# Attention scores of a cycle split three and one around P.V, in place of two and two

## Chip, cores and metric

One NeuronCore of a Trainium2 chip runs the whole program. The metric is the device time of one execution in microseconds (us). Engines are named PE (TensorE matmuls), PEld (its weight loads), ACT (ScalarE), DVE (VectorE), POOL (GpSimd) and SP (SyncE, which here only issues DMAs).

## What is computed

The reference takes x of 8 x 2048 tokens with 256 features and applies three residual blocks: half a routed feed-forward block on 128 picked tokens, an attention over all tokens, and the routed block again. The change touches the attention alone:

```
xh = x.reshape(b, s, 8, 32)                       # after a layer norm
q, k, v = lowrank(xh, Uq, Vq, bq), lowrank(...k), lowrank(...v)
scores = einsum('bqhd,bkhd->bhqk', q, k) / 32 ** 0.5
attn = softmax(scores, axis=-1)
out = einsum('bhqk,bkhd->bqhd', attn, v)
```

Everything is float32.

## The kernel before, in words

The function `attend` (line 1293) works in 64 units, 8 for each of 8 batches. A unit is 4 heads and 512 query tokens, against all 2048 keys. The keys come in 16 chunks of 128. A unit therefore has 64 score tiles, numbered j = 0 to 63, each a matmul of 128 keys by 512 queries for one head (function `score`, matmul on line 1792). Four tiles, the four heads of one chunk, make a **cycle**, and 16 cycles make a unit.

For each tile:

- PE writes the score to one of three PSUM banks (`ps_s`, `RINGS = 3`, line 1261 ff.). The function `score_banks` (line 1264) deals the banks out in turn when the program is written, and remembers for each user who had the bank before (`AFTER`). `after_last` (line 1719) makes PE wait for that user: for an ordinary tile j this is the exponential of tile j - 3.
- ACT takes the exponential of the tile into SBUF (`probs`, line 1682).
- When all four heads of chunk i - 1 are there, PE multiplies them with the values and adds into `ps_acc` (function `pv`, line 1761, eight matmul instructions). It waits for the exponential of tile 4i - 1, the last tile of the cycle before.
- POOL adds the exponentials of the chunks up (`pool_sum`, line 1541), partly after DMAs that add one chunk onto another (line 1520).

Beside this, in each cycle, PE makes four scores of a later unit only for their maximum (`max_four`, line 1795, matmuls on line 1715, four at once in four row groups). DVE reduces three of them (line 1571), ACT copies the fourth out of PSUM (`copy_max`, line 1634) and DVE reduces the copy (line 1573).

The order on PE is written out by hand. In cycle i it is: score(j), score(j + 1), then P.V of chunk i - 1, then score(j + 2), score(j + 3), then the four max scores, with j = 4i. Engines take their instructions in this order, so a waiting instruction holds all behind it. Some cycles carry more:

- Cycle 0: P.V is that of the last chunk of the previous unit. ACT then copies the finished `ps_acc` (`copy_acc`, line 1669), which it does behind the exponential of tile 1. P.V of cycle 1 waits for this copy.
- Cycle 6 (`CLOSE_IN`): behind P.V, PE sums the previous unit's `pool_sum` over the partitions into a bank of `ps_s` (`close_z`, line 1771), for which it waits for POOL's last addition. ACT copies the sums (`copy_z`, line 1675), behind the exponential of tile 25, and PE transposes that copy behind its last score of the cycle (`turn_z`, line 1778). DVE inverts them (line 1586).
- Cycle 7 (`NORM_IN`): behind P.V, PE transposes the copied accumulator (`turn_o`, line 1785), and DVE scales it (line 1602). The bank is held from cycle 6 until tile 34, so that scores turn over in two banks for a while.
- Cycle 13 (`TURN_MAX_IN`): behind the first two scores PE transposes the next unit's maxima (`turn_max`, line 1733) into a bank, and ACT copies them (line 1641).

In the last unit no max scores are left to make, since they run ahead by four cycles and a unit.

Of the kernel before, what the change touches and what calls it, by code (L numbers as in the profile page):

```python
# [1253 lines left out]
NCYC = 16  # L1254
# [3 lines left out]
CLOSE_IN = 6  # L1258
NORM_IN = 7
TURN_MAX_IN = 13  # L1260
RINGS = 3


def score_banks(units, tiles, per_cyc):

    order, last, bank, after = list(range(RINGS)), {}, {}, {}

    def use(user, k):
        bank[user], after[user], last[k] = k, last.get(k), user

    def take(user):
        k = order.pop(0)
        order.append(k)
        use(user, k)

    take((-1, "m"))
    for unit in range(units):  # L1280
        for j in range(tiles):
            if unit > 0 and j == CLOSE_IN * per_cyc + 2:
                use((unit, "z"), order.pop(0))
            if unit > 0 and j == (NORM_IN + 1) * per_cyc + 2:
                order.insert(0, bank[unit, "z"])
            take((unit, j))
            if unit + 1 < units and j == TURN_MAX_IN * per_cyc + 1:
                take((unit, "m"))
    use((units, "z"), order[0])
    return bank, after  # L1290


def attend(nc, tag, qk, v_dram, out):
# [18 lines left out]
    PER_CYC = TILES // NCYC  # L1312
# [5 lines left out]
    ADDS = len(pool_chunks) - 1  # L1318
    ND = len(DMA_PAIRS)
    BANK, AFTER = score_banks(B * BU, TILES, PER_CYC)  # L1320

    def slot(unit, c):

        return (unit * NC + c) % RING

    def adds_through(c):

        return max(pool_chunks.index(c), 1)

    with ExitStack() as ctx:  # L1330
# [5 lines left out]
        def psum(name, shape):  # L1336
            return ctx.enter_context(nc.psum_tensor(f"{tag}_{name}", shape, F32))
# [21 lines left out]
        ps_max = psum("ps_max", [P, HG, 512])  # L1359
        ps_s = psum("ps_s", [P, RINGS, UQ])  # L1360
        ps_acc = psum("ps_acc", [P, UQ])


        def ps_close(unit):

            return ps_s[:, BANK[unit + 1, "z"]]
# [260 lines left out]
        @block.scalar  # L1627
        def _(act):
            def copy_max(unit, n, first_unit=False):

                act.wait_ge(max_scores, unit * FOURS + n + 1)
                if n >= 2 or not first_unit:
                    act.wait_ge(part_max_done, unit * FOURS + n - 1)
                nc.scalar.copy(max_copy[:, n % 2], ps_max[:, HG - 1]).then_inc(max_copied, 1)  # L1634

            def row_of_max(unit, first_unit=False):
                act.wait_ge(max_turned, unit + 1)
                if not first_unit:

                    act.wait_ge(max_in, unit * 32)  # L1640
                nc.scalar.copy(max_row[:], ps_s[0:HG * QT, BANK[unit - 1, "m"], 0:P]).then_inc(max_row_done, 1)

            for n in range(FOURS):
                copy_max(0, n, first_unit=True)
            row_of_max(0, first_unit=True)
            for n in range(MAX_LEAD):
                copy_max(1, n)

            def batch(b, first_batch=False, last=False):
                for un in range(BU):  # L1650
                    unit = b * BU + un
                    carry = un > 0 or not first_batch

                    def free(c):

                        before, k = divmod(unit * NC + c - RING, NC)
                        act.wait_ge(pv_done, before * NC + k + 1)
                        if k in pool_chunks:
                            act.wait_ge(pool_added, before * ADDS + adds_through(k))
                        if k in dma_sources:  # L1660
                            d = before * ND + dma_sources.index(k)
                            act.wait_ge(dma_added[d % MERGES_OUT], (d // MERGES_OUT + 1) * 16)

                    def copy_acc(n):
                        act.wait_ge(pv_done, n * NC)
                        if un > 1 or not first_batch:

                            act.wait_ge(o_turned, n - 1)
                        nc.scalar.copy(oT[:], ps_acc[:]).then_inc(oT_done, 1)

                    def copy_z(n):
                        act.wait_ge(z_done, n)
                        if un > 1 or not first_batch:
                            act.wait_ge(z_turned, n - 1)
                        nc.scalar.copy(zT[:], ps_close(n - 1)).then_inc(zT_done, 1)

                    for j in range(TILES):
                        c, h = divmod(j, HG)
                        if h == 0 and (carry or c >= RING):
                            free(c)  # L1680
                        act.wait_ge(scores, unit * TILES + j + 1)
                        nc.scalar.activation(probs[:, slot(unit, c), h], ps_s[:, BANK[unit, j]], ACT.Exp, scale=SCALE  # L1682
                                             ).then_inc(exp_done, 1)
                        if carry and j == 1:
                            copy_acc(unit)
                        if carry and j == CLOSE_IN * PER_CYC + 1:
                            copy_z(unit)
                        if j == TURN_MAX_IN * PER_CYC + 1 and (un + 1 < BU or not last):
                            row_of_max(unit + 1)
                        if h == HG - 1:  # L1690
                            ahead = un + 1 + (c + MAX_LEAD) // FOURS
                            if ahead < BU or not last:
                                copy_max(unit + ahead - un, (c + MAX_LEAD) % FOURS)
                if last:
                    copy_acc(b * BU + BU)
                    copy_z(b * BU + BU)

            batch(0, first_batch=True)
            for b in range(1, B - 1):
                batch(b)  # L1700
            batch(B - 1, last=True)


        @block.tensor
        def _(pe):
# [13 lines left out]
            def after_last(unit, w):  # L1719

                if AFTER[unit, w] is None:
                    return
                before, x = AFTER[unit, w]
                if x == "z":
                    pe.wait_ge(o_done, before)
                elif x == "m":
                    pe.wait_ge(max_row_done, before + 2)
                else:
                    pe.wait_ge(exp_done, before * TILES + x + 1)

            def turn_max(unit):
                pe.wait_ge(neg_max_done, unit + 1)
                nc.tensor.transpose(ps_s[0:HG * QT, BANK[unit - 1, "m"], 0:P], neg_max[:], ident[:]).then_inc(max_turned, 1)
# [14 lines left out]
            def batch(b, first_batch=False, last=False):  # L1748
                for un in range(BU):
                    unit = b * BU + un  # L1750
                    carry = un > 0 or not first_batch
# [36 lines left out]
                    def score(j):  # L1788
                        c, h = divmod(j, HG)
                        rows = slice(0, LAST_ROW[h])  # L1790
                        after_last(unit, j)
                        nc.tensor.matmul(ps_s[:, BANK[unit, j]], ks[rows, g, h, c * P:(c + 1) * P], qs[rows, unit % NQB, h, :],  # L1792
                                         start=True, stop=True).then_inc(scores, 1)
# [15 lines left out]
                    pe.wait_ge(max_in, unit * 32 + 32)  # L1809
                    for i in range(NCYC):  # L1810
                        j = i * PER_CYC
                        score(j)
                        score(j + 1)
                        if i == TURN_MAX_IN and turns:
                            after_last(unit, "m")
                            turn_max(unit + 1)
                        if i > 0:
                            pe.wait_ge(exp_done, unit * TILES + j)
                            pv(unit, un, i - 1)
                        elif carry:  # L1820
                            pe.wait_ge(exp_done, unit * TILES)
                            pv(unit - 1, (un - 1) % BU, NC - 1)
                        if carry and i == CLOSE_IN:
                            close_z(unit - 1, (un - 1) % BU)
                        if carry and i == NORM_IN:
                            turn_o(unit)
                        score(j + 2)
                        score(j + 3)
                        if carry and i == CLOSE_IN:
                            turn_z(unit)  # L1830
                        max_four(i)
# [8 lines left out]
            for b in range(1, B - 1):  # L1840
                batch(b)
# [60 lines left out]
```

## Time and profile before

| | |
|---|---|
| median of 3 runs | 4373.87 us (4372.24 to 4378.55) |
| the profiled execution | 4375.15 us |
| its span, first to last instruction | 4373.6 us |
| mean granted clock of TensorE | 0.935 |
| busy over the span: PE, DVE, ACT, POOL | 3589.1, 3267.7, 3208.9, 2938.5 us |
| scores, line 1792: PE busy | 1523.4 us in 4096 matmuls |
| P.V, line 1761: PE busy | 1091.8 us in 8192 matmuls |
| exponentials, line 1682: ACT busy | 2262.1 us in 4096 |

The attention's units run from about 830 to 3820 us of the span. Busy time is the union of the recorded instructions of an engine; ends of matmuls are modelled, so a busy PE may still have room. "Idle before" is the time an engine stood still ahead of an instruction, with what ended it. That attribution is inferred: an instruction that waited for a semaphore is put down to whoever raised it, even where it had been raised long before. A row of the time-ordered view begins with the start and the length in us; equal instructions that follow each other are merged into one row with their count.

### The profile page before, as it was taken

What the parts mean: (1) busy time and instruction counts of PE and PEld (TensorE: products, weight loads), DVE (VectorE), ACT (ScalarE), POOL (GpSimd) and SP (SyncE); (2) the same over time, 40 slices, a digit from 0 to 9 for tenths busy, and PEclk for the clock granted to TensorE, in tenths of its full rate; (3) what the DMA queues carried; (4) which work ended last, traced back from release to release, by engine and by line L of the source; (5) the groups of instructions that cost most, each with busy time, mean ns of one, the idle gap of its engine ahead of it and who ended that gap; (6) DMA issues with size and microseconds to landing.
All of it is one profiled execution on the core that took longest, in us unless ns stands there. A gap on an engine that the chain in (4) does not pass through costs nothing. (4 is left out here: it accounts for less than half of the span.)

```text
span 4373.6 us, 59760 instructions
## 1 busy us (share of the span) xinstructions
PE 3589.1 (82%) x20178; PEld 1423.8 (33%) x20178; DVE 3267.7 (75%) x4504; ACT 3208.9 (73%) x6587; POOL 2938.5 (67%) x1094
## 2 busy tenths in 40 slices
PE   0167685599999999999999999999999999900376
PEld 0133463233333333333333333333333333300243
DVE  9644575788888888888888888888888888368544
ACT  5044474498898998998998898998988988723143
POOL 0011000399999999999999999999999999952211
PEclk9998898699999999999999999999999999955588
DMA  8200699689999999999999999999999998877100
GB/s 280 89 3 5 212 395 341 130 180 192 208 199 205 206 199 205 198 209 203 200 208 195 207 198 205 206 199 207 197 208 204 201 205 186 169 249 249 39 5 5
DMA packets 335171, 809.45 MB, mean 185 GB/s; under 512 B 27084, under 2 KB 210912, under 8 KB 271136
## 3 DMA queue, kind: packets, MB, share of 16 engines
q0 software_dynamic: 66432, 475.04, 53.9%
q1 hardware_dynamic: 222496, 284.46, 22.2%
q10 hardware_dynamic: 45952, 46.27, 3.0%
q8 instruction: 159, 2.61, 0.2%
q14 instruction: 132, 1.08, 0.1%
HBM read 198.90 MB, written 136.48 MB: 77 GB/s over the span
## 5 line engine op out<-in xcount | busy, mean ns | idle before, releaser
L1682 ACT ACTIVATE at_probs<-at_ps_s 128x512 f32<-128x512 f32 x4096 | 2262.1, 615 | 254.7 <-PE at_ps_s L1792 247.3
L1541 POOL TENSOR_TENSOR at_pool_sum<-at_pool_sum,at_probs 128x2048 f32<-128x2048 f32 x448 | 2173.0, 4850 | 30.9 <-DMA at_probs<-at_probs 23.5
L1571 DVE TENSOR_REDUCE at_part_max<-at_ps_max 128x3 f32<-128x1536 f32 x1024 | 1801.3, 1759 | 426.8 <-PE at_ps_max L1715 426.7
L1792 PE MATMUL at_ps_s<-at_qs,at_ks 97*128 97x512 f32 (+1 forms) x4096 | 1523.4, 451 | 6.2 <-ACT at_probs L1682 4.9
L1761 PE MATMUL at_ps_acc<-at_probs,at_v 128*32 128x512 f32 x8192 | 1091.8, 605 | 0.9 <-ACT at_probs L1682 0.9
L1792 PEld LDWEIGHTS at_ps_s<-at_qs,at_ks 97*128 97x128 f32 (+1 forms) x4096 | 626.1, 188 | 1102.4 <-ACT at_probs L1682 815.9
L1573 DVE TENSOR_REDUCE at_part_max<-at_max_copy 128x1 f32<-128x512 f32 x1024 | 692.1, 676 | 0.0
L1634 ACT COPY at_max_copy<-at_ps_max 128x512 f32<-128x512 f32 x1024 | 610.1, 596 | 102.2 <-PE at_ps_max L1715 102.1
L1715 PE MATMUL at_ps_max<-at_ks,at_qs 32*128 32x512 f32 x4096 | 525.4, 500 | 83.0 <-DMA at_ks<-qk_parts 49.3
L1520 POOL DMA_DIRECT2D at_probs<-at_probs x448 | 399.3, 891 | 284.5 <-ACT at_probs L1682 236.7
L1715 PEld LDWEIGHTS at_ps_max<-at_ks,at_qs 32*128 32x128 f32 x4096 | 197.8, 183 | 442.1 <-issue 386.0
L1541 POOL TENSOR_TENSOR at_pool_sum<-at_probs 128x2048 f32<-128x2048 f32 x64 | 312.8, 4888 | 0.1
L1761 PEld LDWEIGHTS at_ps_acc<-at_probs,at_v 128*32 128x32 f32 x8192 | 161.2, 108 | 346.1 <-ACT at_probs L1682 299.3
L278 PE MATMUL s_pt<-s_ident,s_sall 128*128 128x128 f32 x2 | 0.9, 446 | 273.9 <-DVE s_sall L222 273.9
L1504 POOL MEMSET at_ones<- 128x128 f32 x1 | 0.2, 204 | 287.2 <-POOLq L62 287.2
L259 ACT ACTIVATE s_y<-s_x,s_small 128x256 f32<-128x256 f32 x256 | 129.2, 587 | 74.4 <-DVE s_small L213 67.0
L660 POOL TENSOR_TENSOR f_att<-f_att,f_rowsum 128x1280 f32<-128x1280 f32 x16 | 49.5, 3097 | 180.0 <-DVE f_rowsum L752 180.0
L815 ACT ACTIVATE f_small<-f_small 128x4 f32<-128x4 f32 x4 | 0.8, 204 | 206.3 <-DVE f_small L714 206.3
L1586 DVE RECIPROCAL at_rz<-at_ps_s 128x16 f32<-128x16 f32 x64 | 16.5, 258 | 170.9 <-PE at_ps_s L1778 170.9
L848 ACT ACTIVATE f_att<-f_att,f_rowmax 128x128 f32<-128x128 f32 x256 | 98.7, 387 | 44.7 <-DVE f_rowmax L748 44.7
L1234 PE MATMUL pr_pqk<-pr_xT,pr_w 128*128 128x512 f32 x256 | 119.4, 610 | 11.9 <-ACT pr_xT L1181 10.8
L159 POOL TENSOR_TENSOR s_x<-s_x,s_add 128x1024 f32<-128x1024 f32 x32 | 74.3, 2342 | 69.4 <-DMA s_add<-attention 69.4
(193 smaller groups left out, 2550.0 us busy)
## 6 DMA issues: line engine op xcount, KB each, us to landing
at_probs<-at_probs POOLq DMA_DIRECT2D x448, 1024.0 KB, 8.3
qk_parts<-pr_hi SPq DMA_DIRECT2D x32, 1024.0 KB, 12.0
qk_parts<-pr_lo SPq DMA_DIRECT2D x32, 1024.0 KB, 12.5
at_qs<-qk_parts SPq DMA_DIRECT2D x320, 64.0 KB, 5.8
at_ks<-qk_parts SPq DMA_DIRECT2D x80, 256.0 KB
s_x<-in_x SPq DMA_DIRECT2D x16, 1024.0 KB
after_ffn<-s_y ACTq DMA_DIRECT2D x16, 1024.0 KB, 6.8
v_tokens<-pr_v SPq DMA_DIRECT2D x32, 512.0 KB, 11.0
```

The source lines that it names most:

```text
L259: last = nc.scalar.activation(yb[:, k, t, :], xb[:, k, t, :], ACT.Identity, scale=sm[:, k, 0, t:t + 1], bias=sm[:, k, 1, t:t + 1])
L848: last = nc.scalar.activation(att[:, s, h], att[:, s, h], ACT.Exp, scale=ATT_SCALE, bias=rowmax[:, s, h:h + 1], accum_out=rowsum[:, s, h:h ...
L1234: nc.tensor.matmul(pqk[:, m, :], w[:, m // NG, m % NG, :], xT[:, n % 2, m % NG, :], start=True, stop=True).then_inc(qk_done, 1)
L1520: nc.gpsimd.dma_start(probs[:, slot(unit, a)], probs[:, slot(unit, c)], accum_op=ALU.add).then_inc(dma_added[(unit * ND + d) % MERGES_OUT] ...
L1541: nc.gpsimd.tensor_tensor(acc, first, probs[:, slot(unit, c)], ALU.add).then_inc(pool_added, 1)
L1571: nc.vector.reduce_max(part_max[:, 0:HG - 1, t, c], ps_max[:, 0:HG - 1], AX.X).then_inc(three_max_done, 1)
L1573: nc.vector.reduce_max(part_max[:, HG - 1:HG, t, c], max_copy[:, n % 2:n % 2 + 1], AX.X).then_inc(part_max_done, 1)
L1634: nc.scalar.copy(max_copy[:, n % 2], ps_max[:, HG - 1]).then_inc(max_copied, 1)
L1682: nc.scalar.activation(probs[:, slot(unit, c), h], ps_s[:, BANK[unit, j]], ACT.Exp, scale=SCALE).then_inc(exp_done, 1)
L1715: last = nc.tensor.matmul(ps_max[:, h], qs[rows, unit % NQB, h, t * P:(t + 1) * P], ks[rows, un % BU // NU, h, c * 512:(c + 1) * 512], sta ...
L1761: last = nc.tensor.matmul(ps_acc[h * DH:(h + 1) * DH, :], v[:, k // NU, c, h * DH:(h + 1) * DH], probs[:, slot(n, c), h], start=(c == 0), ...
L1792: nc.tensor.matmul(ps_s[:, BANK[unit, j]], ks[rows, g, h, c * P:(c + 1) * P], qs[rows, unit % NQB, h, :], start=True, stop=True).then_inc( ...
```

## The change

The number of scores in front of P.V becomes a table `SPLIT`: 3 in all cycles but 7, 8 and 13, where it stays 2. The bank of the sums is dealt out, and the copies `copy_acc` and `copy_z` are placed on ACT, behind the last score in front of P.V, which now is tile 2 of cycle 0 and tile 26 in cycle 6.

```diff
@@ -1258,6 +1258,8 @@
 TURN_MAX_IN = 13
+
+SPLIT = tuple(2 if i in (CLOSE_IN + 1, NORM_IN + 1, TURN_MAX_IN) else 3 for i in range(NCYC))
 RINGS = 3
@@ -1279,7 +1281,7 @@
-            if unit > 0 and j == CLOSE_IN * per_cyc + 2:
+            if unit > 0 and j == CLOSE_IN * per_cyc + SPLIT[CLOSE_IN]:
                 use((unit, "z"), order.pop(0))
@@ -1681,9 +1683,9 @@
-                        if carry and j == 1:
+                        if carry and j == SPLIT[0] - 1:
                             copy_acc(unit)
-                        if carry and j == CLOSE_IN * PER_CYC + 1:
+                        if carry and j == CLOSE_IN * PER_CYC + SPLIT[CLOSE_IN] - 1:
                             copy_z(unit)
@@ -1809,8 +1811,8 @@
                         j = i * PER_CYC
-                        score(j)
-                        score(j + 1)
+                        for t in range(SPLIT[i]):
+                            score(j + t)
                         if i == TURN_MAX_IN and turns:
@@ -1824,8 +1826,8 @@
                             turn_o(unit)
-                        score(j + 2)
-                        score(j + 3)
+                        for t in range(SPLIT[i], PER_CYC):
+                            score(j + t)
                         if carry and i == CLOSE_IN:
```

## Rows read from the trace of the kernel before

**Rows 1.** Stretch; busy us of PE, PEld, DVE, ACT, POOL (count); clock; DMA share, GB/s

```profile
848.00:3700.00 2852.00, 2845.41 (x16642) 1004.31 (x16645) 2361.43 (x2134) 2559.91 (x5065) 2621.27 (x915) 1.00 0.96 201
```

**Rows 2.** Weight loads in order of time over one ordinary cycle: start, length, line

```profile
2309.38 0.30 PEld L1792 LDWEIGHTS at_ps_s<-at_qs,at_ks 97*128 97x128 f32 x2 [0.84 <-ACT at_probs L1682]
2310.05 0.19 PEld L1715 LDWEIGHTS at_ps_max<-at_ks,at_qs 32*128 32x128 f32 x4 [0.37 <-DVE at_part_max L1571]
2310.49 0.30 PEld L1792 LDWEIGHTS at_ps_s<-at_qs,at_ks 97*128 97x128 f32 x2 [0.25 <-issue]
2311.15 0.16 PEld L1761 LDWEIGHTS at_ps_acc<-at_probs,at_v 128*32 128x32 f32 x8 [0.36 <-ACT at_probs L1682]
2312.14 0.30 PEld L1792 LDWEIGHTS at_ps_s<-at_qs,at_ks 97*128 97x128 f32 x2 [0.84 <-ACT at_probs L1682]
```

**Rows 3.** ACT in order of time over the same cycle

```profile
2309.92 1.09 ACT L1682 ACTIVATE at_probs<-at_ps_s 128x512 f32<-128x512 f32 x2 [0.20 <-PE at_ps_s L1792]
...
2311.36 1.12 ACT L1682 ACTIVATE at_probs<-at_ps_s 128x512 f32<-128x512 f32 x2
2312.68 0.60 ACT L1682 ACTIVATE at_probs<-at_ps_s 128x512 f32<-128x512 f32 x1 [0.20 <-PE at_ps_s L1792]
```

**Rows 4.** Weight loads in the last unit, the loads of P.V

```profile
3815.65 0.16 PEld L1761 LDWEIGHTS at_ps_acc<-at_probs,at_v 128*32 128x32 f32 x8 [0.30 <-ACT at_probs L1682]
...
3818.31 0.16 PEld L1761 LDWEIGHTS at_ps_acc<-at_probs,at_v 128*32 128x32 f32 x8 [0.30 <-ACT at_probs L1682]
```

**Rows 5.** PE in the last unit: second and third score of a run

```profile
3816.98 0.40 PE L1792 MATMUL at_ps_s<-at_qs,at_ks 128*128 128x512 f32 x1
...
3817.22 0.40 PE L1792 MATMUL at_ps_s<-at_qs,at_ks 97*128 97x512 f32 x1
```

**Rows 6.** Weight loads of a cycle 6, up to the first scores of cycle 7

```profile
1826.69 0.30 PEld L1792 LDWEIGHTS at_ps_s<-at_qs,at_ks 97*128 97x128 f32 x2 [0.25 <-issue]
...
1829.21 0.30 PEld L1792 LDWEIGHTS at_ps_s<-at_qs,at_ks 97*128 97x128 f32 x2 [0.84 <-ACT at_probs L1682]
1829.99 0.42 PEld L1778 LDWEIGHTS at_ps_s<-at_ident,at_zT 128*128 128x128 f32 x4 [0.48 <-ACT at_zT L1675]
...
1831.01 0.30 PEld L1792 LDWEIGHTS at_ps_s<-at_qs,at_ks 97*128 97x128 f32 x2 [0.25 <-ACT at_probs L1682]
```

**Rows 7.** PE in the same cycle 6: the sums over the partitions

```profile
1828.24 1.04 PE L1771 MATMUL at_ps_s<-at_pool_sum,at_ones 128*32 128x512 f32 x8
```

**Rows 8.** ACT in the same cycle 6: the copy of the sums

```profile
1829.35 0.59 ACT L1675 COPY at_zT<-at_ps_s 128x512 f32<-128x512 f32 x1 [0.66 <-PE at_ps_s L1771]
```

**Rows 9.** Weight loads in cycle 8: score 33, then P.V

```profile
1834.74 0.19 PEld L1792 LDWEIGHTS at_ps_s<-at_qs,at_ks 97*128 97x128 f32 x1 [0.30 <-ACT at_probs L1682]
1835.17 0.16 PEld L1761 LDWEIGHTS at_ps_acc<-at_probs,at_v 128*32 128x32 f32 x8 [0.25 <-issue]
```

**Rows 10.** Around a cycle 1: weight loads at its start, P.V and cycle 2; ACT's exponentials 2 and 3

```profile
2327.18 0.45 PEld L1792 LDWEIGHTS at_ps_s<-at_qs,at_ks 97*128 97x128 f32 x2 [0.24 <-issue]
2327.93 0.16 PEld L1761 LDWEIGHTS at_ps_acc<-at_probs,at_v 128*32 128x32 f32 x8 [0.30 <-ACT at_probs L1682]
...
2330.04 0.19 PEld L1792 LDWEIGHTS at_ps_s<-at_qs,at_ks 97*128 97x128 f32 x1 [0.25 <-issue]
...
2326.73 1.15 ACT L1682 ACTIVATE at_probs<-at_ps_s 128x512 f32<-128x512 f32 x2
```

**Rows 11.** The copy of P.V's sum: two units in a row, and all 64 (first and last start)

```profile
2279.59 0.63 ACT L1669 COPY at_oT<-at_ps_acc 128x512 f32<-128x512 f32 x1
...
2326.26 0.63 ACT L1669 COPY at_oT<-at_ps_acc 128x512 f32<-128x512 f32 x1
...
L1669 ACT COPY at_oT<-at_ps_acc x64: 586/629/632, 877.1 to 3822.1; 128x512 f32<-128x512 f32 x64
```

**Rows 12.** PE in a cycle 6 whose sums waited for POOL

```profile
2437.79 0.64 PE L1771 MATMUL at_ps_s<-at_pool_sum,at_ones 128*32 128x512 f32 x4 [1.21 <-POOL at_pool_sum L1541]
```

**Rows 13.** Who waited for whom between 700 and 3700 us: total, times, longest

```profile
PEld at_ps_s L1792 <- ACT at_probs L1682: 772.3, 1038, 1.7
```

## The prediction

> **What bounds the kernel now.** I began with the busy time of the stretch in which the attention runs at the full granted clock: of 2852 us PE is busy for 2845, POOL for 2621, ACT for 2560 and DVE for 2361 [rows 1]. Clock 1.00 there means its upper level, 2.4 GHz. A busy PE may still stand in a loop with ACT, so I went to single cycles. The weight loads tell where PE is, because the load of a new kind of matmul goes out only when the work before it has run through. From the load of one score pair to the next kinds: 0.67 us to the four max scores, 0.44 to the next pair, 0.66 to P.V, 0.99 (two decimals of 0.996) to the next pair, 2.76 in all [rows 2]. ACT beside it starts an operation every 0.48 us (2309.92 to 2311.36 is three of them) and then stands idle for 0.20 us until a score comes [rows 3].
>
> Two things could hold P.V: PE's own sequence, or the exponential of the tile just before. That exponential ends at 2309.92 + 1.09 = 2311.01 [rows 3]. A released load follows an end on ACT by 0.05 us: the copy of the sums ends at 1829.94, the transpose that waits for it loads at 1829.99 [rows 7, 8]. So P.V could have loaded at 2311.06; it did at 2311.15 [rows 2]. The loop P.V, score pair, two exponentials, P.V has 0.09 us to spare, and PE's sequence is the bound. The last unit, which has no max scores, confirms it: with 0.44 less work its cycle is still 2.66 us (P.V to P.V) [rows 4], and 0.54 (load to exponential) + 1.09 + 0.05 + 0.99 = 2.67 is just that loop. **The loop is 2.67, PE's sequence is 2.76.** The chain that ended last is of no help here, for it stays in the stage behind.
>
> **The change, part by part.** It adds and removes no instruction. In 13 of 16 cycles the third score is moved from behind P.V to in front of it. DMAs and the queues of SP, POOL and DVE keep their order; on ACT two copies move by one exponential.
>
> *Steady cycle, PE.* There are still four switches of kind. Three scores cost a pair and one more: 0.66 + 0.24, the 0.24 being the start of a third score after the second, 3816.98 to 3817.22, where nothing held it [rows 5]. A lone score up to the next kind costs 0.43: score 33, released late, loads at 1834.74, and P.V loads at 1835.17 [rows 9]. So the new cycle is 0.90 + 0.99 + 0.43 + 0.44 = 2.76, and the old one 0.66 + 0.99 + 0.67 + 0.44 = 2.76. The gain of a third score in a run, 0.24, is what the pair behind P.V loses. Rounding leaves -0.02 to +0.02; I enter +0.005, since the third weight load cannot begin before the second score streams, which the pair does not suffer. A rule of the Trainium skill speaks the other way: "TensorE: Matmul & The Clock Gate", section "Wait — 56ns, not 53.3ns?", gives 215.7 ns between matmuls of 512 columns at the full clock, where the row here has 0.24; by it the cycle would be about 0.02 shorter rather than 0.005 longer.
>
> *Steady cycle, waits.* Set zero at the load of the lone score. Max scores load at 0.43, the next run at 0.87, its second score starts at 1.20 (0.33 more), and the third may load then. It reuses the bank of the lone score and needs its exponential, which starts at 0.54, lasts 0.60 and releases at 1.19 [rows 2, 3]. That is just in time, and P.V (at 1.77) would be late only if that load came after 1.77 - 0.43 = 1.34. So nothing is gated; ACT needs 5 x 0.48 = 2.40 of 2.76. The loop between the engines shrinks to 1.19 + 0.43 + 0.99 = 2.61, which is worth nothing while PE needs 2.76.
>
> *Cycles 9 and 14*, which follow a cycle still split two and two. Count from the load of that pair. The second exponential of the pair ends at 2311.01 - 2309.38 = 1.63 and releases at 1.68 [rows 2, 3]. The third score may only load then, and P.V comes at 1.68 + 0.43 = 2.11. Today it comes at 0.67 + 0.44 + 0.66 = 1.77. Of the 0.34 the lone score behind it gives back 0.24. Each of the two costs 0.10: +0.20 a unit.
>
> *Cycle 6.* The third score goes in front of P.V and so in front of the sums of the previous unit (line 1771). Today, from the first load at 1826.69: sums at 1.55, turned sums at 3.30, cycle 7 at 4.32 [rows 6]. From sums to turned sums are 1.75 us, of which two scores cover 0.97 to 1.64 and the rest is waiting: sums end at 1829.28, ACT's copy runs from 1829.35 to 1829.94 [rows 7, 8]. That chain is the path; it now starts 0.24 later, with one score instead of two beneath it, so PE idles for 1.75 - 0.97 - 0.43 = 0.35. Cycle 7 starts at 4.56: +0.24 a unit. Behind the copy on ACT the exponential of score 27 waits; its readers come in cycle 7, later than it.
>
> *Cycle 1.* Today the copy of P.V's sum sits in front of exponentials 2 and 3; they end at 2326.73 + 1.15 = 2327.88, P.V of cycle 1 loads at 2327.93, and the cycle lasts 2.86, 0.10 over [rows 10]. With the copy behind exponential 2, exponential 3 is the sixth operation behind that of the lone score of cycle 15: it starts 0.54 + 6 x 0.48 = 3.42 after that score's load, lasts 1.15 - 0.48 = 0.67 and releases at 4.14; P.V comes at 4.14 + 0.43 = 4.57 against 4.53 unheld. 0.04 to 0.10 over goes: I take -0.08 a unit.
>
> *POOL.* Units repeat in 46.67 us when quiet, and in 46.75 on the mean over 63 [rows 11]: 5 us in all, where the sums waited for POOL's last addition, 1.21 us in the one shown [rows 12]. POOL's chain keeps its length, the sums ask for it 0.24 later, and the cycles between are longer: I take back 4 us (0 to 5).
>
> Cycles 7, 8 and 13 stay. *Sum.* Ten ordinary cycles +0.05, cycle 1 -0.08, cycle 6 +0.24, cycles 9 and 14 +0.20: +0.41 a unit, for 62 units +25.4. The first has nothing to close, +0.25. The last is bound by the loop, 14 x (2.61 - 2.66) + 0.24 = -0.5. Less 4 for POOL: **+21 us**. The profiled execution took 4375.15 us around a span of 4373.6; the median of the runs shown is 4373.87, so the sum stands 1.3 above it, and I count from the median: 4395 us.
>
> **Rivals.** *The moved score is cheaper (no change).* If the third score in a run costs 0.22 and not 0.24, within the reading of two rows, 13 x 64 = 832 cycles give back 0.02 each, 17 us: 4378. For it: the rule above; against: [rows 5]. Chance 0.14.
>
> *The loop was the bound after all (faster).* The profile puts 772 us of idle time before score loads down to ACT [rows 13], and ACT waits 0.20 a cycle for a score [rows 3]. If P.V's release were what sets its load, the cycle would fall to 2.61: 0.15 in 10 cycles of 63 units is 95 us, less the 25 of the special cycles: about 4305. Against it stands the 0.09 us between release and load; it decides if a release takes 0.14 and not 0.05. A smaller form is that the waits of cycles 6, 9 and 14 are covered while cycle 1 and POOL give their 9: 4365. Together 0.11, the small form likelier.
>
> *The third score is held in every cycle (much slower).* P.V has 0.15 us to spare; if the lone score's exponential came 0.20 late, 0.05 in 10 cycles of 63 units adds 32 us: 4427. Chance 0.05.
>
> **How the numbers follow.** Forecast 4395, chance 0.70, with its terms from 4383 to 4412: the steady term alone is +-0.02 x 630 = +-13, cycles 9 and 14 lie between 0 and twice their price. The range 4372 to 4412 adds the no-change case and leaves out the two ends. 0.2% is 8.7 us, about what a measurement of this kernel can tell from no change: faster ends at 4365, slower begins at 4383. Slower is the forecast and the held score, 0.75; same is the cheap third score and a little of the faster case, 0.16; the rest of that, 0.09, is faster.
>
> **What would show it.** In the changed profile: ordinary cycles at 2.76 to 2.77; lone score load to max load 0.43; cycles 9 and 14 at 2.86; in cycle 6 a weight load on line 1778 with some 0.6 us of idle time before it put down to the copy on ACT, and 4.56 us for the cycle; cycle 1 under 2.81; ACT with one idle gap of 0.35 a cycle. I am wrong if ordinary cycles fall below 2.74, or if cycle 6 stays at 4.32.

## The result, and the profile after

The changed kernel takes 4390.84 us (median of 7 runs, 4388.46 to 4392.39), against 4373.68 for the kernel before (7 runs beside it): a ratio of 1.0040, 95% interval 1.0029 to 1.0052. It is 17 us slower; the forecast was 21.

In what follows a cycle's time is the distance from the weight load of its first score to that of the next cycle's first score, and a table gives the median over units 1 to 61 (counted from 0) of one profiled execution. In the changed kernel the lines of the attention lie two higher (score 1794, P.V 1763, exponential 1684, transposes of the sums 1780).

The weight loads of an ordinary cycle of the changed kernel (start, length, engine, line; idle time before, with its releaser), to be read against [rows 2]:

```profile
1852.33 0.53 PEld L1794 LDWEIGHTS at_ps_s<-at_qs,at_ks 97*128 97x128 f32 x3 [0.25 <-issue]
1853.23 0.16 PEld L1763 LDWEIGHTS at_ps_acc<-at_probs,at_v 128*32 128x32 f32 x8 [0.37 <-issue]
1854.22 0.19 PEld L1794 LDWEIGHTS at_ps_s<-at_qs,at_ks 128*128 128x128 f32 x1 [0.84 <-ACT at_probs L1684]
1854.65 0.19 PEld L1717 LDWEIGHTS at_ps_max<-at_ks,at_qs 32*128 32x128 f32 x4 [0.24 <-issue]
1855.09 0.53 PEld L1794 LDWEIGHTS at_ps_s<-at_qs,at_ks 97*128 97x128 f32 x3 [0.25 <-issue]
```

The run of three takes 0.90 us, P.V 0.99, the lone score 0.43, the max scores 0.44: 2.76, what it was. The three loads stand in one row of 0.53 us with no gap, so the third was not held. Note the row of the lone score: 0.84 us of idle time put down to the exponential, in a cycle in which PE never waited. It is the time P.V's matmuls took.

ACT in the same cycle, against [rows 3]:

```profile
1852.96 1.60 ACT L1684 ACTIVATE at_probs<-at_ps_s 128x512 f32<-128x512 f32 x3
1854.76 0.60 ACT L1684 ACTIVATE at_probs<-at_ps_s 128x512 f32<-128x512 f32 x1 [0.21 <-PE at_ps_s L1794]
1855.26 0.58 ACT L1636 COPY at_max_copy<-at_ps_max 128x512 f32<-128x512 f32 x1
1855.72 1.60 ACT L1684 ACTIVATE at_probs<-at_ps_s 128x512 f32<-128x512 f32 x3
```

ACT does four exponentials and the copy without a gap between 1854.76 and 1857.32 and then waits 0.20 us for the lone score (I had 0.35, since I took 0.48 an operation and left out that the last one is recorded longer). The wait now stands in front of the lone score, where it stood in front of the pair behind P.V; it is as long as it was.

Cycle 6, the loads of PE, against [rows 6]:

```profile
1835.89 0.53 PEld L1794 LDWEIGHTS at_ps_s<-at_qs,at_ks 97*128 97x128 f32 x3 [0.24 <-issue]
...
1838.64 0.19 PEld L1794 LDWEIGHTS at_ps_s<-at_qs,at_ks 128*128 128x128 f32 x1 [0.84 <-ACT at_probs L1684]
1839.42 0.42 PEld L1780 LDWEIGHTS at_ps_s<-at_ident,at_zT 128*128 128x128 f32 x4 [0.59 <-ACT at_zT L1677]
1840.00 0.19 PEld L1717 LDWEIGHTS at_ps_max<-at_ks,at_qs 32*128 32x128 f32 x4 [0.17 <-issue]
1840.44 0.30 PEld L1794 LDWEIGHTS at_ps_s<-at_qs,at_ks 97*128 97x128 f32 x2 [0.24 <-issue]
```

The lone score would have let the next kind load at 1838.64 + 0.43 = 1839.07; the transposes load at 1839.42, held by the copy of the sums for 0.35 us. The cycle lasts 4.55 in place of 4.32 us. On line PE the same place reads:

```profile
1837.67 1.04 PE L1773 MATMUL at_ps_s<-at_pool_sum,at_ones 128*32 128x512 f32 x8
...
1839.42 0.66 PE L1780 MATMUL at_ps_s<-at_ident,at_zT 128*128 128x128 f32 x4 [0.28 <-ACT at_zT L1677]
```

Cycle 9, the first split three and one behind cycle 8, which is split two and two, as weight loads:

```profile
1845.60 0.30 PEld L1794 LDWEIGHTS at_ps_s<-at_qs,at_ks 97*128 97x128 f32 x2 [0.84 <-issue]
...
1846.70 0.30 PEld L1794 LDWEIGHTS at_ps_s<-at_qs,at_ks 97*128 97x128 f32 x2 [0.25 <-issue]
1847.27 0.19 PEld L1794 LDWEIGHTS at_ps_s<-at_qs,at_ks 97*128 97x128 f32 x1 [0.27 <-ACT at_probs L1684]
1847.70 0.16 PEld L1763 LDWEIGHTS at_ps_acc<-at_probs,at_v 128*32 128x32 f32 x8 [0.25 <-issue]
...
1849.57 0.30 PEld L1794 LDWEIGHTS at_ps_s<-at_qs,at_ks 97*128 97x128 f32 x2 [0.24 <-issue]
```

Here the run of three breaks into two rows: two loads, a gap, and the third at 1847.27, which is 1.67 us behind the load of cycle 8's last pair. The cycle lasts 2.87.

All cycles together, with what the prediction said (a unit has nine cycles in the first line, not the ten I counted):

| cycles | before | after | change in a unit | predicted |
|---|---|---|---|---|
| 0, 2 to 5, 10 to 12, 15 | 24.83 | 24.83 | 0.00 | +0.05 |
| 1 | 2.86 | 2.77 | -0.09 | -0.08 |
| 6 | 4.32 | 4.55 | +0.23 | +0.24 |
| 7, 8 | 6.25 | 6.26 | +0.01 | 0 |
| 9 | 2.77 | 2.87 | +0.11 | +0.10 |
| 13 | 2.91 | 2.88 | -0.03 | 0 |
| 14 | 2.77 | 2.86 | +0.10 | +0.10 |
| mean of cycle 6 less its median (POOL late) | 0.09 | 0.02 | -0.08 | -0.06 |
| mean unit | 46.78 | 47.03 | +0.25 | +0.35 |

61 units by 0.245 us are 14.9, and from the first to the last score load of the attention the trace has 2991.8 us before and 3006.6 after. The other 2.3 us of the 17.1 between the two spans lie in stages that the edit does not touch (3.4 more ahead of the attention, 1.1 less behind it), in one execution of each kernel. No run says why they differ.

The last unit, which has no max scores, runs faster than before, as P.V's loads show against the 2.66 of [rows 4]:

```profile
3834.04 0.16 PEld L1763 LDWEIGHTS at_ps_acc<-at_probs,at_v 128*32 128x32 f32 x8 [0.25 <-ACT at_probs L1684]
...
3836.65 0.16 PEld L1763 LDWEIGHTS at_ps_acc<-at_probs,at_v 128*32 128x32 f32 x8 [0.25 <-ACT at_probs L1684]
```

2.61 us, the shortened loop. The first fifteen cycles of that unit take 41.67 us together, 0.39 less than before.

### The profile page after: what moved, and what is told of

Same layout as the page of the kernel before. It is cut to its first block and busy times, and to the rows that moved or that the text cites. A ratio compares the mean times of both kernels' runs of the same rounds, so it can differ in the third digit from the quotient of the medians.

```text
span 4390.7 us, 59760 instructions
## 1 busy us (share of the span) xinstructions
PE 3596.3 (82%) x20178; PEld 1475.0 (34%) x20178; DVE 3265.9 (74%) x4504; ACT 3211.0 (73%) x6587; POOL 2934.9 (67%) x1094
## 3 DMA queue, kind: packets, MB, share of 16 engines
q8 instruction: 159, 2.61, 0.2%
## 5 line engine op out<-in xcount | busy, mean ns | idle before, releaser
L1794 PEld LDWEIGHTS at_ps_s<-at_qs,at_ks 97*128 97x128 f32 (+1 forms) x4096 | 678.8, 188 | 1164.5 <-ACT at_probs L1684 850.7
```

## The experiments

**My theory**: the cycle is held by PE's own sequence; the change costs only where a wait has no cover (cycle 6, and a run of three behind a cycle split two and two). **The rivals**: each moved score costs a little everywhere (17 us over 832 cycles); or the loop between PE and ACT is the bound. Medians per cycle (us), and the times; the ratio of each run is to runs of the kernel before made beside it (4373.4 to 4375.0 on the median):

| run | 0 | 1 | 6 | 7 | 8 | 9 | 13 | 14 | mean unit | time | ratio to before (95%) |
|---|---|---|---|---|---|---|---|---|---|---|---|
| before | 2.75 | 2.86 | 4.32 | 3.24 | 3.01 | 2.77 | 2.91 | 2.77 | 46.78 | 4373.7 | |
| after | 2.76 | 2.77 | 4.55 | 3.25 | 3.01 | 2.87 | 2.88 | 2.86 | 47.03 | 4390.8 | 1.0040 (1.0029 to 1.0052) |
| e1 | 2.76 | 2.77 | 4.32 | 3.24 | 3.00 | 2.86 | 2.88 | 2.86 | 46.80 | 4377.5 | 1.0006 (0.9997 to 1.0015) |
| e2 | 2.87 | 2.94 | 4.56 | 3.24 | 3.01 | 2.77 | 2.91 | 2.77 | 47.16 | 4397.7 | 1.0057 (1.0043 to 1.0070) |
| e3 | 2.76 | 2.76 | 4.31 | 3.24 | 3.01 | 2.76 | 2.85 | 2.76 | 47.09 | 4395.6 | 1.0052 (1.0039 to 1.0066) |
| e4 | 2.76 | 2.77 | 4.00 | 3.24 | 3.01 | 2.86 | 2.88 | 2.86 | 46.48 | 4355.1 | 0.9954 (0.9941 to 0.9968) |
| e5 | 2.67 | 2.94 | 4.23 | 3.23 | 2.84 | 2.67 | 2.90 | 2.64 | 45.86 | 4310.1 | 0.9856 (0.9836 to 0.9876) |
| e6 | 2.61 | 2.93 | 4.40 | 3.24 | 2.83 | 2.86 | 2.70 | 2.86 | 45.46 | 4284.8 | 0.9798 (0.9780 to 0.9816) |
| e7 | 2.76 | 2.85 | 4.32 | 3.16 | 2.76 | 2.76 | 2.91 | 2.76 | 46.43 | 4356.8 | 0.9959 (0.9945 to 0.9973) |
| e8 | 2.75 | 2.85 | 4.02 | 3.28 | 3.01 | 2.77 | 2.90 | 2.77 | 46.50 | 4358.6 | 0.9960 (0.9946 to 0.9975) |
| e9 | 2.77 | 2.85 | 4.02 | 3.20 | 2.76 | 2.76 | 2.90 | 2.76 | 46.17 | 4338.0 | 0.9913 (0.9899 to 0.9926) |
| e10 | 2.77 | 2.85 | 4.02 | 3.42 | 2.77 | 2.76 | 2.90 | 2.76 | 46.40 | 4352.3 | 0.9945 (0.9930 to 0.9960) |
| e11 | 2.77 | 2.85 | 4.32 | 3.24 | 3.01 | 2.75 | 2.91 | 2.76 | 46.67 | 4361.7 | 0.9969 (0.9956 to 0.9981) |

### e1: cycle 6 undone

```diff
-SPLIT = tuple(2 if i in (CLOSE_IN + 1, NORM_IN + 1, TURN_MAX_IN) else 3 for i in range(NCYC))
+SPLIT = tuple(2 if i in (CLOSE_IN, CLOSE_IN + 1, NORM_IN + 1, TURN_MAX_IN) else 3 for i in range(NCYC))
```

> The changed kernel, but cycle 6 split two and two again (nine, ten and so on as changed). Theory (PE's own sequence is the bound; the change costs only where a wait is uncovered): cycle 6 back from 4.55 to 4.32 us, all other cycles as in the changed kernel (cycle 1 2.77, cycles 9 and 14 2.87); 63 units by 0.23 is 14 us, so about 4377 us. Rival (each moved score costs a little, 17 us over 832 cycles, 0.02 each): a thirteenth of the loss goes, about 4389 us.

Measured 4377.5: 13 us of the 17 hung on one cycle of the thirteen. Cycle 6 went back to 4.32, and no other median moved by more than 0.01. An equal price for each moved score is out.

### e2: only cycles 0 to 6

```diff
+SPLIT = tuple(3 if i <= CLOSE_IN else 2 for i in range(NCYC))
```

> Three and one in cycles 0 to 6 only, two and two in 7 to 15. Theory: the late third score moves with the place where a cycle split three and one follows one split two and two, from cycles 9 and 14 to cycle 0. Cycles 9 and 14 2.76, cycle 0 2.86 where it was 2.76, cycle 1 2.77, cycle 6 4.55. Against the kernel before +0.10 - 0.09 + 0.23 = +0.24 a unit, 15 us, less 2 to 3 for POOL: about 4386 us. Rival (0.02 per moved score): 7 x 64 x 0.02 = 9 us, 4383 us, and cycle 0 at 2.78.

Measured 4397.7, not 4386. The late third score did move to cycle 0 (2.87), as expected, and cycles 9 and 14 are back at 2.77. But cycle 1 rose to 2.94, where I had 2.77: with the same copy in the same new place, it lost 0.08 against the kernel before instead of gaining 0.09. So the new place alone does not bring the gain. In e2 cycle 15 ends in a pair again, and ACT reaches cycle 0 later: its first exponential there starts 0.87 us behind the first score's load, where it is 0.63 in the changed kernel, and cycle 0 is 0.11 longer. The third score of cycle 1 waits for exponential 3:

```profile
2247.56 0.68 ACT L1684 ACTIVATE at_probs<-at_ps_s 128x512 f32<-128x512 f32 x1
...
2247.65 0.30 PEld L1794 LDWEIGHTS at_ps_s<-at_qs,at_ks 97*128 97x128 f32 x2 [0.24 <-issue]
2248.29 0.19 PEld L1794 LDWEIGHTS at_ps_s<-at_qs,at_ks 97*128 97x128 f32 x1 [0.34 <-ACT at_probs L1684]
```

The exponential ends at 2248.24 and the load follows at 2248.29, 0.64 behind that of the pair; in the changed kernel it is 0.49.

### e3: five cycles, each behind a cycle split two and two

```diff
+SPLIT = tuple(3 if i in (2, 4, 10, 12, 15) else 2 for i in range(NCYC))
```

> Three and one in cycles 2, 4, 10, 12 and 15, two and two elsewhere, so that each of the five follows a cycle split two and two. Theory: each of the five lasts 2.86 us in place of 2.76, five by 64 by 0.10 is 32 us: about 4406 us, more than the whole change costs with only five moved scores. Rival (0.02 per moved score): 5 x 64 x 0.02 = 6 us, 4380 us. A second rival (the loop between PE and ACT is the bound and the third score shortens it): the five fall under 2.75 and the time under 4374 us.

Measured 4395.6: five moved scores cost more than thirteen. The medians of the five cycles are 2.86, 2.86, 2.86, 2.86 and 2.86, 0.10 each, which neither rival allows. The time fell short of 4406 because cycle 1 is 2.76 (0.10 less) and cycle 13 is 2.85 (0.06 less), and POOL was late less often (mean less median of cycle 6 is 0.04). Cycle 0 is split two and two here, so the copy sits in its old place; what precedes it is cycle 15 with a lone last score. The weight loads of its cycle 1 against [rows 10]:

```profile
1819.99 0.36 PEld L1794 LDWEIGHTS at_ps_s<-at_qs,at_ks 97*128 97x128 f32 x2 [0.25 <-issue]
1820.66 0.16 PEld L1763 LDWEIGHTS at_ps_acc<-at_probs,at_v 128*32 128x32 f32 x8 [0.31 <-ACT at_probs L1684]
```

Here P.V loads 0.67 behind the scores, where it was 0.75. ACT's first exponential of cycle 0 starts 0.63 behind the first score's load (0.87 in the kernel before). ACT then stands idle 0.06 us in front of the copy, which waits for P.V, and exponentials 2 and 3 take 1.09 us together, where it was 1.15. So with the copy in its old place, and cycle 0 split two and two, a cycle 15 that ends in a lone score is enough for the gain.

### e4: the changed kernel, transposes behind the max scores

```diff
-                        if carry and i == CLOSE_IN:
-                            turn_z(unit)
                         max_four(i)
+                        if carry and i == CLOSE_IN:
+                            turn_z(unit)
```

> The changed kernel with the transposes of the sums (cycle 6) behind the four max scores in place of in front of them. Theory (in cycle 6 PE idles 0.35 us for ACT's copy of the sums): the max scores cover the wait, the transposes load 0.44 us after the max scores, and cycle 6 lasts 4.21 us in place of 4.55; 63 by 0.33 is 21 us, about 4370 us, under both kernels. Rival: DVE, which inverts the sums ahead of its next maximum in its own order, starts that maximum 0.9 us later, and the max scores of cycle 7 wait for it: cycle 7 grows by what cycle 6 gains, 4385 to 4391 us.

Measured 4355.1, 36 us under the changed kernel and 19 under the one before. Cycle 6 fell by 0.54, more than the 0.33 expected, and cycle 7 did not move, so the rival of DVE's queue has nothing here:

```profile
1827.33 0.19 PEld L1794 LDWEIGHTS at_ps_s<-at_qs,at_ks 128*128 128x128 f32 x1 [0.84 <-ACT at_probs L1684]
1827.75 0.19 PEld L1717 LDWEIGHTS at_ps_max<-at_ks,at_qs 32*128 32x128 f32 x4 [0.24 <-issue]
1828.19 0.42 PEld L1780 LDWEIGHTS at_ps_s<-at_ident,at_zT 128*128 128x128 f32 x4 [0.25 <-ACT at_zT L1677]
1828.58 0.30 PEld L1794 LDWEIGHTS at_ps_s<-at_qs,at_ks 97*128 97x128 f32 x2
```

The max scores fill the wait of 0.35. The rest is the switch: from the transposes to scores takes 0.39 us here, and it had been 0.58 to the max scores.

### e5 and e6: a shorter sequence of PE under both kernels

```diff
+                    wide = 512 if first_unit else 128
-                    last = nc.tensor.matmul(ps_max[:, h], qs[...], ks[rows, ..., c * 512:(c + 1) * 512], ...)
+                    last = nc.tensor.matmul(ps_max[:, h, 0:wide], qs[...], ks[rows, ..., c * 512:c * 512 + wide], ...)
...
-                nc.gpsimd.tensor_tensor(acc, first, probs[:, slot(unit, c)], ALU.add).then_inc(pool_added, 1)
+                heads = HG if unit < 2 else HG // 2
+                nc.gpsimd.tensor_tensor(acc[:, 0:heads], first[:, 0:heads], probs[:, slot(unit, c), 0:heads], ALU.add
+                                        ).then_inc(pool_added, 1)
```

> The kernel before, with two things left out so that PE's sequence is no longer the longest: from the second unit on the max scores take 128 of their 512 keys (PE's sequence loses 384 columns a cycle, about 0.16 us: 2.60), and from the third unit on POOL adds two of four heads (POOL needs 45 of 46.7 us a unit and would else be the next bound). Theory: ordinary cycles fall to 2.67 us, the loop of P.V, score pair and two exponentials, and no further, some 4305 us. Rival (PE's sequence and the loop do not differ): they fall to 2.60.

> The changed kernel with the same two things left out. Theory: ordinary cycles fall to 2.61 us, the shortened loop, so that the same change that costs 17 us in the full kernel now gains: as in the last unit (sum of its cycles 41.7 after, 42.1 before) 0.4 a unit, 25 us under the run before it. Rival (each moved score costs 0.02 whatever the bound is): 17 us over it.

Measured 4310.1 and 4284.8: the change now gains 25 us. The four runs of each spread wider than elsewhere (4302.7 to 4320.7 and 4278.2 to 4293.7), but do not overlap. Ordinary cycles are 2.67 and 2.61, the two loops. The loads of an ordinary cycle of e5:

```profile
1812.16 0.44 PEld L1795 LDWEIGHTS at_ps_s<-at_qs,at_ks 97*128 97x128 f32 x2
1812.90 0.16 PEld L1764 LDWEIGHTS at_ps_acc<-at_probs,at_v 128*32 128x32 f32 x8 [0.30 <-ACT at_probs L1684]
...
1814.83 0.19 PEld L1795 LDWEIGHTS at_ps_s<-at_qs,at_ks 97*128 97x128 f32 x1
```

and of e6:

```profile
1813.25 0.30 PEld L1797 LDWEIGHTS at_ps_s<-at_qs,at_ks 97*128 97x128 f32 x2
1813.75 0.19 PEld L1797 LDWEIGHTS at_ps_s<-at_qs,at_ks 97*128 97x128 f32 x1 [0.20 <-ACT at_probs L1686]
...
1815.87 0.19 PEld L1797 LDWEIGHTS at_ps_s<-at_qs,at_ks 97*128 97x128 f32 x1
```

In e5 the pair's loads take 0.44 us instead of 0.30 and P.V follows 0.74 behind the first load instead of 0.66: held by ACT. In e6 the third load stands alone, held as well. So the loop is there, and it is the bound only once PE's sequence is shorter than it. The size needs care. The sum of the cycles' medians differs by 0.16 us a unit, about 10 us; the other 14 or so are two long waits of PE in e5 in front of the first max scores of a new head group, in cycle 12 of units 26 and 34 (8.0 and 10.0 us for that cycle), against one (5.9 us) in e6, and what follows them. In the two or three cycles behind such a wait the granted clock is near its lower level (1.2 GHz; 1.00 is 2.4 GHz), and they take 4.2 to 4.8 us each. The stretches behind the two waits of e5, with the clock third from the end:

```profile
2053.16:2066.86 13.70, 13.70 (x53) 4.51 (x49) 7.05 (x6) 7.57 (x15) 3.27 (x2) 0.52 0.50 102
2430.05:2439.07 9.02, 9.02 (x37) 3.03 (x33) 4.70 (x4) 4.84 (x10) 3.27 (x2) 0.53 0.24 49
```

PE had been idle for 5.1 and 7.1 us ahead of them. Wait and slow cycles together come to 10.8 us in each of the two units of e5, and to 7.1 in e6 (3.1 us idle, then a clock of 0.51). The profile puts the wait of e6 down to the DMA of new keys, those of e5 to nothing. That the total met the expected 25 is partly chance.

### e7: the bank of the sums back at tile 32

```diff
-            if unit > 0 and j == (NORM_IN + 1) * per_cyc + 2:
+            if unit > 0 and j == (NORM_IN + 1) * per_cyc:
```

> The kernel before, with the bank of the sums given back to the scores at tile 32 in place of 34, so that score 32 waits for DVE's scaling (ended 34.12 in the unit of rows 6 to 9) and no longer for exponential 30 (34.20), and score 33 for nothing new. Theory: the waits of rows 9 go, cycle 8 falls from 3.01 to 2.76 us and cycle 7 from 3.24 to 3.16, 63 by 0.33 is 21 us, about 4353 us. Rival (PE's pair behind the transposes is slow by itself): no change, 4374 us.

Measured 4356.8, with cycles 7 and 8 at 3.16 and 2.76. The two held scores of [rows 9] have become an unbroken pair, released by DVE:

```profile
1827.22 0.30 PEld L1792 LDWEIGHTS at_ps_s<-at_qs,at_ks 97*128 97x128 f32 x2 [0.26 <-DVE at_o L1602]
1827.88 0.16 PEld L1761 LDWEIGHTS at_ps_acc<-at_probs,at_v 128*32 128x32 f32 x8 [0.37 <-ACT at_probs L1682]
```

### e8: the edit of e4 in the kernel before

> The kernel before, with the transposes of the sums behind the four max scores. Theory: cycle 6 falls from 4.32 to 4.02 us (0.11 of waiting, and the transposes give way to scores 0.17 sooner than to max scores, as the run with the changed kernel showed), 63 by 0.30 is 19 us, about 4355 us: the same as the changed kernel with this edit, since the max scores now cover ACT's copy in both. Rival (the split three and one is what makes the edit pay): about 4368 us.

Measured 4358.6, cycle 6 at 4.02. With the max scores as cover it hardly matters how many scores stand behind the sums (4.00 in e4): the 0.23 that the change cost in cycle 6 was the uncovered part of ACT's copy, to within 0.02.

### e9 and e10: both edits, and where DVE inverts

Both have the edits of e7 and e8. e9 also lets DVE invert the sums behind its first maximum of cycle 6:

```diff
-                        if carry and i == CLOSE_IN:
-                            invert(unit - 1)
...
-                            part_max_of(unit + ahead - un, (i + MAX_LEAD) % FOURS)
+                            part_max_of(unit + ahead - un, (i + MAX_LEAD) % FOURS,
+                                        between=(lambda: invert(unit - 1)) if closes else None)
...
```

> The kernel before, split two and two, with the bank given back at tile 32, the transposes of the sums behind the max scores, and DVE's inversion of the sums moved behind its first maximum of cycle 6. Theory: the two gains add, since DVE scales the outputs about when score 32 wants the bank: cycle 6 4.02, cycle 7 3.2 to 3.3, cycle 8 2.76 us, 0.50 to 0.58 under the 10.57 of these three now; 63 by 0.53 is 33 us, about 4341 us. Rival (POOL, 45 of 46.7 us a unit, becomes the bound as units fall to 46.15): cycle 6 is held in more units, about 4350 us.

> As the last one, but with DVE's inversion in its old place, ahead of the maximum of cycle 6. Theory: DVE, in order, waits for the late transposes with that maximum queued behind, and reaches the scaling some 0.5 us later (about 7.7 us after the start of cycle 6 in place of 7.4); score 32 waits for it: cycle 7 grows to about 3.7 us, cycle 8 stays 2.76, and most of the gain is lost: about 4369 us. Rival (DVE has room): as the last one, 4341 us.

Measured 4338.0 and 4352.3. e9 beats both kernels: 0.9913 of the one before, 53 us under the changed one. It has the first's split, two and two. POOL did not become the bound: the sums wait for it no more than they did (mean less median of cycle 6 is 0.09, as before). e10 loses 14 of the 37 us, by the place of one short instruction in DVE's queue. DVE around cycle 7 of e10:

```profile
1827.33 0.26 DVE L1586 RECIPROCAL at_rz<-at_ps_s 128x16 f32<-128x16 f32 x1 [1.86 <-PE at_ps_s L1778]
1827.51 1.70 DVE L1571 TENSOR_REDUCE at_part_max<-at_ps_max 128x3 f32<-128x1536 f32 x1
1829.12 0.67 DVE L1573 TENSOR_REDUCE at_part_max<-at_max_copy 128x1 f32<-128x512 f32 x1
1829.70 0.68 DVE L1602 TENSOR_TENSOR at_o<-at_ps_s,at_rz 128x512 f32<-128x512 f32 x1
```

DVE sits idle for 1.86 us in front of the inversion, and scales at 1829.70; PE's score 32 waits until 1830.44, the start of cycle 8, so that cycle 7 takes 3.42. In e9 the scaling starts at 1820.90 in a unit whose cycle 6 starts at 1814.43, 6.47 behind; in e10 it is 1829.70 - 1823.00 = 6.70. I had put 3.7 on cycle 7: the mechanism is there, but half as large, because I added the recorded lengths (1.76 and 0.68), while DVE starts these operations 1.61 and 0.58 apart.

### e11: POOL at half its work

The POOL part of the edit of e5 alone, in the kernel before.

> The kernel before with POOL adding two of four heads from the third unit on; the rest of the sums is left out. Theory (units over 46.69 us waited for POOL in cycle 6): every unit falls to 46.69, 0.09 by 62 is 5 us, about 4368 us. Rival (what makes these units long is the loading of new keys and values, not POOL): 4374 us with cycle 6 still above 4.4 on the mean.

Measured 4361.7: 13 us, not 6. The first part is as expected: every cycle 6 is at 4.32, mean and median alike, and units 2 to 62 take 7.0 us less. The second I had not seen. Behind the last score the attention ends on POOL, first in the kernel before, then in e11:

```profile
3837.58 1.93 PE L1771 MATMUL at_ps_s<-at_pool_sum,at_ones 128*32 128x512 f32 x8 [15.53 <-POOL at_pool_sum L1541]
```

```profile
3823.10 1.94 PE L1773 MATMUL at_ps_s<-at_pool_sum,at_ones 128*32 128x512 f32 x8 [9.45 <-POOL at_pool_sum L1542]
```

The wait is 6 us shorter, which with the 7 makes the 13.

## Why the prediction was right, point by point

- **What bounds the kernel.** PE's sequence at 2.76 against a loop of 2.67: right. The ordinary cycles kept their time, and e5 showed the loop at 2.67 once PE had less to do.
- **The ordinary cycle.** Predicted +0.005, measured 0.00 over nine cycles. The third score in a run costs the 0.24 of [rows 5] and the lone one 0.43, as read. That the sum comes out at 0.00 and not at +0.005 is below what the two decimals of the terms can tell. The rule of the Trainium skill ("TensorE: Matmul & The Clock Gate", section "Wait — 56ns, not 53.3ns?", 215.7 ns a matmul) would have made the cycle 0.02 shorter. The trace does not agree here: a run of three takes 0.90 us where a pair took 0.66.
- **The loop shrinks to 2.61** and is worth nothing while PE needs 2.76: right in both halves, the first by the last unit and e6, the second by the ordinary cycles.
- **Cycles 9 and 14**, +0.10 each: measured +0.11 and +0.10, the third load 1.67 behind the pair's where I had 1.68; e3 gave 0.10 five times over.
- **Cycle 6**, +0.24: measured +0.23. e1, e4 and e8 confirm place and cause.
- **Cycle 1**, -0.08: measured -0.09, and the step holds. It counted six operations of ACT from the lone score of cycle 15 to exponential 3, and so rested on two things, the lead that this score gives ACT and the copy's new place. The trace of the changed kernel has the six:

```profile
1819.01 0.60 ACT L1684 ACTIVATE at_probs<-at_ps_s 128x512 f32<-128x512 f32 x1 [0.20 <-PE at_ps_s L1794]
...
1821.41 0.63 ACT L1671 COPY at_oT<-at_ps_acc 128x512 f32<-128x512 f32 x1
1821.88 0.67 ACT L1684 ACTIVATE at_probs<-at_ps_s 128x512 f32<-128x512 f32 x1
...
1822.59 0.19 PEld L1794 LDWEIGHTS at_ps_s<-at_qs,at_ks 97*128 97x128 f32 x1 [0.20 <-ACT at_probs L1684]
1823.02 0.16 PEld L1763 LDWEIGHTS at_ps_acc<-at_probs,at_v 128*32 128x32 f32 x8 [0.24 <-issue]
```

  Exponential 3 starts 2.87 behind that of the lone score, six times 0.48, ends at 1822.55 and lets the third score load 0.04 later; P.V comes 0.92 behind the pair's load where 0.90 would be unheld. My expectation for e2 kept the place and forgot the lead. e3 has the lead without the place. No run has the changed splits with the copy in its old place. There the copy would wait for a P.V that loads 0.24 later than in e3, and exponentials 2 and 3 would both stand behind it. From the 1.13 us between P.V's load and the copy in e3, exponential 3 would start some 0.45 us later than it does, an estimate. So in the changed kernel the place is needed as well.
- **Cycle 13** I left at zero; it fell by 0.03. e3 has it too (2.85), where cycle 12 ends in a lone score. The loads from the transpose of the maxima on show what went, first in the kernel before, then in the changed one:

```profile
1848.88 0.09 PEld L1733 LDWEIGHTS at_ps_s<-at_ident,at_neg_max 128*16 128x16 f32 x1 [0.28 <-ACT at_probs L1682]
...
1850.08 0.45 PEld L1792 LDWEIGHTS at_ps_s<-at_qs,at_ks 97*128 97x128 f32 x2 [0.84 <-ACT at_probs L1682]
```

```profile
1858.19 0.09 PEld L1735 LDWEIGHTS at_ps_s<-at_ident,at_neg_max 128*16 128x16 f32 x1
...
1859.61 0.30 PEld L1794 LDWEIGHTS at_ps_s<-at_qs,at_ks 97*128 97x128 f32 x2 [0.84 <-ACT at_probs L1684]
```

  The transpose waited for an exponential, and the two loads behind P.V took 0.45 us instead of 0.30; with ACT's lead out of cycle 12 neither is held. No run took the two apart.
- **POOL**, -4 us: measured -0.08 in 61 units, 5 us. It took back nearly all that was lost, 0.09 a unit or nearly 6 us; I had read 5, from a mean that takes in the shorter last unit.
- **The sum** was +21 for the attention and is 14.8. The largest miss is the ordinary cycle (3 us: a rounding guess, and ten cycles for nine), then cycle 13 (2 us), POOL and cycle 6 (1 us each). The whole came out at 17, closer to 21, by the 2.3 us from stages that the edit does not touch; that part is luck.

The faster rival fell by the ordinary cycles; the one of a cheaper third score too, and with it the case of no change; the held third score occurs in no ordinary cycle.

## What to carry to other kernels

Before reordering an in-order queue, work out two numbers for the cycle: the engine's own sequence, switches of kind included, and the longest loop of waits through it. An order that shortens the loop is worth nothing while the sequence is longer, and it costs at the seams: where a rarely run chain (here sums, copy, transposes) loses its cover, and where an old cycle meets a new one. Look at the seams first for gains as well: three small edits at two of them were worth 37 us here, more than twice what thirteen moved scores cost.

## What the runs showed that I had not expected

- A PE switch from transposes to scores took 0.39 us and to the four max scores 0.58, so the order of kinds seems to have a price of its own (0.19 of the 0.54 us that e4 gained in cycle 6; e8 shows the 0.39 in the kernel before).
- Idle time of the weight loads put down to ACT rose from 772 us [rows 13] to 801 in the changed kernel, while PE waits for ACT in none of its ordinary cycles. e5, whose P.V is truly held by ACT, has the same kind of row. What separates the two is the distance from ACT's end to the load (0.05 us when it releases), not the label.
- The last unit ends with 15.5 us of PE idle for POOL's last additions. Beyond e11 no run bears on it.
